# A four-layer attention kernel: the opening is rearranged, three biases move into columns, and the attention values are taken 64 queries at a time

## The chip, the cores and the metric

The kernel runs on one core of a Trainium2 chip. The metric is the device time of one execution in microseconds (us). The engines are named as the profile names them: PE is TensorE (PEld its weight loads), DVE is VectorE, ACT is ScalarE, POOL is GpSimd, SP is SyncE, which here only issues transfers.

## What is computed

`x` is 16 batches of 64 tokens with 128 features; `ctx_1024` is a second sequence of the same shape. Four blocks follow each other, all with 16 heads of 8 features, in f32:

```
L0: x = ln1(x + selfattn(x));  x = ln2(x + crossattn(x, ctx, every 4th key));  x = ln3(x + W2 gelu(W1 x + b1) + b2)
L1: q = x Ws + bs;  kv = ctx Wt + bt (keys are also the values);  a = attn(q, kv, masked) Wo + bo
    x = ln(x + [x, a] Wu + bu)
L2: x = ln(x + causal attention of x over ctx);  x = x + W2 gelu(W1 x + b1) + b2
L3: x = x + ( relu(q k)^2 in a band around ctx_index, divided by its floored sum ) v Wo,  q and k from rms-normed x and ctx
```

The kernel calls the five attentions sa, ca, l1, l2 and l3, and the two feed-forward parts f and g.

## The kernel before

The 1024 tokens are cut into four groups `g` of 256 (4 batches). A group has one PSUM bank, `bank[g]`, for everything but scores, and all groups share a four-bank tile `score`. There is no loop over layers. A table `SCHEDULE` lists some 700 steps as `step/layer/group/part`; every engine walks the whole table and does the steps that are its own, waiting on semaphores for what a step reads. So the table sets the order on each engine, and an engine that waits at one step does nothing of the next.

For one attention and group the steps are: `k`, `q`, `v` (PE, projections), `k_kept`, `q_kept` (ACT, bias added and copied to SBUF), `k_heads` and `q_heads` (DVE, four copies with the other heads masked out), `s` (PE, scores with queries on the partitions), `max` (DVE, row maxima), `max_parts` (DVE, the maxima split into two bf16 parts), `m` and `m_row` (PE, ACT: transposed), `t` (PE, the transposed scores, with the maxima subtracted through the `sel` matrix), two `exp` (ACT), two `av`, `divide` (DVE), `flip` and `attT` (transposed back), `z` (PE, output projection and residual, centred), `var`, `rstd` (ACT, POOL), `scale`, `flip_x`, `ln`.

`av` is the function `attend` (L494 on). Probabilities lie in SBUF with keys on the 128 partitions (two batches by the trick of alternating heads) and are the stationary operand; the values, with a column of ones for the denominator, are the moving one: 2 heads of 9 columns, 18 in all. A half of 256 tokens has 16 heads and 2 batches `x` of 64 queries, and each 64 are taken in two pieces `hf` of 32, so one matmul loads a 128x32 block and writes 32 partitions of the bank. One `av` step is 32 such matmuls; each f32 matmul appears as two in the trace, so 64 rows. There are 32 such steps in sa, l1, l2 and l3, and in ca four of 16 matmuls (32 rows) with 72 moving columns.

Three output biases are added in odd ways. `weights(3)` multiplies them through the output matrices into `shift` (three columns: sa, ca, f) and `row` (one row, l1). POOL adds `shift` to the layer's input x in place (`shifted`, 12 operations) before `z` reads it; for l1 a matmul of a row of ones with `row` (f32, 256 columns) opens each `z`.

The opening: SP issues x of group 0, the bias table V, three weight matrices, then x of groups 1 to 3 in one transfer; ACT issues the first two matrices. PE does 6 warm-up matmuls (`WARM`) and four more ahead of the first `s`. POOL zeroes the three value buffers `v_ext` one at a time, each inside its step `v_base`.

Of the kernel before, what the change touches and what calls it, by code (L numbers as in the profile page):

```python
# [10 lines left out]
R = 4  # L11
# [29 lines left out]
WARM = (6, 4)  # L41
# [7 lines left out]
SHIFT = {"sa": 0, "ca": 1, "f": 2}  # L49
W_BANK = {0: 3, 1: 2, 2: 3, 3: 3}  # L50
# [19 lines left out]

def own_readers(k):
# [23 lines left out]
k_heads/sa/3 weights_kept//3/2 m_row/sa/2 exp/sa/0/1 k/l1/1 k_kept/l1/1 t/sa/1 exp/sa/1/1 v/ca/1 av/sa/0/1 v_base/ca
v_even/ca/1 exp/sa/1 patterns divide/sa q_heads/sa/2 ctx_ms weights//3/3 s/sa/3 max/sa/3 weights_kept//3/3 av/sa/1
flip/sa k/ca/2 attT/sa max_parts/sa/3 k_heads/ca/2 k/l1 k_kept/l1 ctx_rs shifted/sa/1 shifted/sa/3 t/sa/2 exp/sa/2
q_heads/sa/3 av/sa/1/1 divide/sa/1 m/sa/3 m_row/sa/3 exp/sa/2/1 weights//2/1 flip/sa/1 shifted/sa z/sa var/sa
attT/sa/1 weights_kept//2/1 av/sa/2 rstd/sa t/sa/3 exp/sa/3 band z/sa/1 var/sa/1 k/ca/3 scale/sa k_heads/l1/1
flip_x/sa k_heads/ca/3 av/sa/2/1 ln/sa exp/sa/3/1 q/ca q_kept/ca rstd/sa/1 scale/sa/1 av/sa/3 flip_x/sa/1 ln/sa/1  # L100
divide/sa/2 v/ca flip/sa/2 v_even/ca attT/sa/2 q/ca/1 q_kept/ca/1 av/sa/3/1 divide/sa/3 s/ca max/ca shifted/sa/2
# [82 lines left out]
def build(nc, a, out):  # L184
# [3 lines left out]
    with ctx:  # L188
# [115 lines left out]
        def _(pe):  # L304
# [27 lines left out]
            def weights(i):  # L332
# [18 lines left out]
                else:  # L351
                    pe.wait_ge(sem("weights_kept"), nth("weights_kept", "", W_BANK[0], 0))
                    pe.wait_ge(sem("v_loaded"), 16)
                    for name, terms in (("sa", [("sa_vb", WC[:, WC_OF["sa"], :]), ("sa_ob", mat("center"))]),
# [3 lines left out]
                        for n, (b, m) in enumerate(terms):  # L358
                            mm(o[:, c:c + 1], m, col(b), start=n == 0, stop=n == len(terms) - 1)
# [732 lines left out]
```

## Time and profile before

| | us |
|---|---|
| median of 3 runs | 202.1 (201.26 to 202.43) |
| the profiled execution | 200.97 |
| its span in the trace | 199.0 |
| PE busy in the span | 180.7 (91%) |
| DVE, ACT, POOL busy | 131.7, 115.4, 47.6 |

The trace is of one execution, 1.1 us under the median. What lies around the span is 2.0 us. PE is busy nearly throughout; its idle time lies mostly in the opening.

### The profile page before, as it was taken

Reading aid. Unit: us, or ns where it says so; the run is one execution under the profiler, and the core shown is the slowest. Engines: PE = TensorE matmul, PEld = TensorE weight load, DVE = VectorE, ACT = ScalarE, POOL = GpSimd, SP = SyncE. Lnnn points to the kernel's source line nnn. Section 1 sums busy time; section 2 is a strip of 40 time slices with the busy share of each in tenths; the row PEclk is TensorE's granted clock in tenths of the full one; section 3 lists DMA queues with packets and bytes.
Section 4 is the critical chain, followed back from the end, with each engine's and each line's share of the span. In section 5 each row is a group of like instructions: output and inputs, shape, how many; then the busy total and the mean of one; then the engine's idle time right before and its main releaser. Section 6 shows DMA issues by size and latency. Waiting matters only on the chain.

```text
span 199.0 us, 10271 instructions
## 1 busy us (share of the span) xinstructions
PE 180.7 (91%) x4556; PEld 135.8 (68%) x4556; DVE 131.7 (66%) x250; ACT 115.4 (58%) x299; POOL 47.6 (24%) x73
## 2 busy tenths in 40 slices
PE   7693999989999999999999999898999999899863
PEld 3261768677878788778767667574667678777753
DVE  0799967986786873297367759634768156578770
ACT  2243348547485884667664566164597595554552
POOL 3793000943351167323101100011100102000000
PEclk9999799999999999999999999999999999999999
DMA  5992000000000000000000000000000000000102
GB/s 122 387 374 101 0 3 7 5 5 3 7 3 3 3 2 3 0 3 3 5 3 3 3 5 7 3 3 3 3 3 3 3 5 3 3 0 3 35 3 79
DMA packets 3899, 6.05 MB, mean 30 GB/s; under 512 B 528, under 2 KB 3216, under 8 KB 3600
## 3 DMA queue, kind: packets, MB, share of 16 engines
q1 hardware_dynamic: 3568, 5.23, 7.6%
q8 instruction: 36, 0.59, 1.2%
q10 hardware_dynamic: 288, 0.17, 0.3%
q14 instruction: 7, 0.06, 0.1%
HBM read 4.88 MB, written 0.52 MB: 27 GB/s over the span
## 4 chain that ended last, share of the span: by engine, by line
PE 67%; DVE 10%; issue 9%; ACT 5%; POOL 5%; DMA 3%; SPq 1%; POOLq 0%; DVEq 0%
PE bank L317 30%; PE score L320 21%; PE bank L320 10%; PE bank L533 4%; DVE m_col_sb L863 3%; DMA xa_sb<-in_xT 3%; ACT probs_sb L675 2%; DVE q_heads_sb L804 2%; POOL xa_sb L990 2%; DVE k_heads_sb L790 1%; DVE m_part_sb L870 1%; POOL xb_sb L990 1%; DVE probs_sb L850 1%; PE bank L443 1%; POOL rstd_sb L997 1%
## 5 line engine op out<-in xcount | busy, mean ns | idle before, releaser
L863 DVE TENSOR_REDUCE m_col_sb<-score 128x32 f32<-128x2048 f32 (+1 forms) x16 | 30.2, 1889 | 9.8 <-PE score L320 9.6
L675 ACT ACTIVATE probs_sb<-score 128x1024 f32<-128x1024 f32 (+1 forms) x28 | 26.4, 962 | 13.1 <-PE score L320 13.0
L317 PEld LDWEIGHTS bank<-v_ext_sb,probs_sb 128*32 128x32 f32 x2176 | 22.7, 110 | 9.6 <-issue 7.1
L317 PE MATMUL bank<-v_ext_sb,probs_sb 128*32 128x18 f32 (+1 forms) x2176 | 26.2, 189 | 1.9 <-DVE floor_sb L940 0.9
L995 POOL TENSOR_SCALAR vare_sb<-var_sb 128x2 f32<-128x2 f32 x20 | 5.5, 277 | 85.5 <-ACT att_sb L727 85.4
L317 PE MATMUL bank<-xa_sb,W_sb 128*128 128x256 f32 x62 | 18.2, 402 | 2.3 <-DMA xa_sb<-in_xT 1.6
L320 PE MATMUL score<-q_heads_sb,k_kept_sb 32*64 32x256 f32 x512 | 19.4, 386 | 0.9 <-DVE q_heads_sb L804 0.9
L927 DVE TENSOR_TENSOR att_sb<-bank,rstd_sb 128x256 f32<-128x256 f32 x20 | 8.4, 422 | 16.2 <-POOL rstd_sb L997 16.2
L740 ACT ACTIVATE hid_sb<-bank,V_sb 128x256 f32<-128x256 f32 x32 | 13.3, 471 | 8.6 <-PE bank L317 8.5
L320 PE MATMUL score<-k_heads_sb,q_kept_sb 32*64 32x256 f32 x384 | 14.3, 390 | 4.2 <-DVE m_col_sb L863 3.2
L727 ACT ACTIVATE att_sb<-bank 128x128 f32<-128x128 f32 x40 | 10.7, 276 | 10.7 <-PE bank L320 10.4
L533 PE MATMUL bank<-W_sb,att_sb 128*128 128x128 f32 x80 | 15.7, 283 | 1.1 <-DVE att_sb L890 0.8
L804 DVE TENSOR_TENSOR q_heads_sb<-q_kept_sb,small_sb 128x1024 f32<-128x1024 f32 x12 | 14.6, 1220 | 3.1 <-ACT q_kept_sb L686 3.0
L997 POOL TENSOR_TENSOR rstd_sb<-vare_sb,half_sb 128x2 f32<-128x2 f32 x20 | 14.3, 717 | 1.7
L317 PEld LDWEIGHTS bank<-xa_sb,W_sb 128*128 128x128 f32 x62 | 10.4, 193 | 5.9 <-issue 3.8
L790 DVE TENSOR_TENSOR k_heads_sb<-k_kept_sb,small_sb 128x1024 f32<-128x1024 f32 x11 | 13.5, 1235 | 1.1 <-ACT k_kept_sb L697 1.0
L317 PE MATMUL bank<-xb_sb,W_sb 128*128 128x256 f32 x48 | 13.8, 396 | 0.4 <-ACT xb_sb L732 0.2
L320 PEld LDWEIGHTS score<-k_heads_sb,q_kept_sb 32*64 32x64 f32 x384 | 7.5, 131 | 8.7 <-DVE m_col_sb L863 3.9
L320 PEld LDWEIGHTS score<-q_heads_sb,k_kept_sb 32*64 32x64 f32 x512 | 12.0, 131 | 2.1 <-issue 1.8
L659 ACT ACTIVATE v_ext_sb<-bank 64x128 f32<-64x128 f32 x32 | 8.8, 274 | 7.8 <-PE bank L317 7.2
L533 PEld LDWEIGHTS bank<-W_sb,att_sb 128*128 128x128 f32 x80 | 9.2, 142 | 5.3 <-DVE att_sb L890 2.1
L850 DVE SCALAR_TENSOR_TENSOR probs_sb<-score,band_sb 128x256 f32<-128x256 f32 x32 | 11.1, 416 | 2.2 <-PE score L320 2.2
(130 smaller groups left out, 354.2 us busy)
## 6 DMA issues: line engine op xcount, KB each, us to landing
W_sb<-in_mats SPq DMA_DIRECT2D x1, 1088.0 KB, 7.8
W_sb<-in_mats SPq DMA_DIRECT2D x1, 1024.0 KB, 9.9
ctxT_sb<-in_ctxT SPq DMA_DIRECT2D x1, 512.0 KB, 5.7
cn_sb<-in_ctx SPq DMA_DIRECT2D x1, 512.0 KB, 11.1
hid_sb<-in_idx SPq DMA_DIRECT2D x1, 512.0 KB, 6.5
out<-attT_sb SPq DMA_DIRECT2D x4, 128.0 KB, 1.8
xa_sb<-in_xT SPq DMA_DIRECT2D x1, 384.0 KB, 5.1
W_sb<-in_mats SPq DMA_DIRECT2D x1, 192.0 KB, 4.4
```

The source lines that it names most:

```text
L317: return pe.matmul(o, l, r, start=start, stop=stop)
L320: return pe.matmul(o, l, r, start=start, stop=True, skip_group_check=True)
L533: last = pe.transpose(o[:, j * 128:(j + 1) * 128], att[:, g, j, :], mat("ident"))
L659: last = act.activation(dst[:, :, 1 - f, :, 0:DH], src[:, :, 1 - f, :].rearrange("p c (h n) -> p c h n", n=DH), ACT.Copy)
L675: act.activation(dst, src, ACT.Exp, scale=SCALE).then_inc(sem("exp"), 1)
L727: last = act.activation(att[:, g, j, :], bank[g][:, j * 128:(j + 1) * 128], ACT.Square, scale=D ** -0.5, accum_out=var[:, g, j:j + 1])
L740: last = act.activation(hid[:, cc, tok(g)], bank[g][:, c * GT:(c + 1) * GT], ACT.Gelu, bias=col(f"{name}_b1_{cc}"), scale=1.0)
L790: dve.tensor_tensor(k_heads[HEADS[name]][:, g, :, :], k_kept[KEYS[name]][:, g, :].unsqueeze(1).to_broadcast([128, HH, GT]), const("head"). ...
L804: last = dve.tensor_tensor(q_heads[:, g, :, :], src.unsqueeze(1).to_broadcast([128, HH, GT]), const("head").unsqueeze(2).to_broadcast([128 ...
L850: last = dve.scalar_tensor_tensor(p, src, 0.0, m, ALU.max, ALU.mult)
L863: dve.tensor_reduce(o, src, AX.X, ALU.max).then_inc(sem("max"), 1)
L997: pool.tensor_tensor(rstd[:, g, :], vare[:, g, :], half[:, 0:NJ], ALU.pow).then_inc(sem("rstd"), 1)
```

## The change

**Values.** The loop over `hf` is gone: one matmul loads 128x64 and writes 64 partitions, so a step has 16 matmuls (32 rows) where it had 32 (64 rows). The same in ca with its 72 columns.

```diff
                     for a_ in range(2):
                         for h in range(HH):
-                            for hf in range(2):
-                                for x in range(2):
-                                    c = 64 * x + 32 * hf
-                                    o = bank[g][c:c + 32, i * 144 + a_ * 72:i * 144 + a_ * 72 + 72]
-                                    last = mm(o.rearrange("p (e h n) -> p e h n", e=2, h=HH)[:, :, h, :],
-                                              p[:, i, x, a_, h, 32 * hf:32 * hf + 32],
-                                              ve[:, x, g * NJ + i, 8 * a_ + h:8 * a_ + 8:HH, :])
+                            for x in range(2):
+                                o = bank[g][64 * x:64 * x + 64, i * 144 + a_ * 72:i * 144 + a_ * 72 + 72]
+                                last = mm(o.rearrange("p (e h n) -> p e h n", e=2, h=HH)[:, :, h, :],
+                                          p[:, i, x, a_, h, :],
+                                          ve[:, x, g * NJ + i, 8 * a_ + h:8 * a_ + 8:HH, :])
```

**Bias columns.** l1's bias becomes a fourth column of `shift`; a new `weights(4)` turns it, split into three bf16 parts, into `row` (3x128 bf16), and carries the ca and f shifts through the next matrices. DVE makes `moved` of it: biases of `ln` (sa, ca), of the f hidden layer and of ca's q. ACT adds them in operations that it does anyway, so POOL's `shifted` remains for sa only.

```diff
-SHIFT = {"sa": 0, "ca": 1, "f": 2}
+SHIFT = {"sa": 0, "ca": 1, "f": 2, "l1": 3}
+MOVED = ["sa_lb", "ca_lb", "f_b1_0", "f_b1_1", "f_b1_2", "f_b1_3", "ca_qb"]
...
-                                        ("f", [("f_b2", mat("center"))])):
+                                        ("f", [("f_b2", mat("center"))]),
+                                        ("l1", [("l1_ob", WC[:, WC_OF["l1_upd"], :]), ("l1_ub", mat("center"))])):
...
-                    mm(o[0:1, 128:256], col("l1_ob"), WC[:, WC_OF["l1_upd"], :], stop=False)
-                    last = mm(o[0:1, 128:256], col("l1_ub"), mat("center"), start=False)
...
+                    pe.transpose(o[0:3, 0:64].bitcast(BF), row_part[:, :], identb[:, :])
+                    for c in range(F_CHUNKS):
+                        mm(o[:, 128 + c:129 + c], mat(f"f_w1_{c}"), shift[:, SHIFT["f"]:SHIFT["f"] + 1])
+                    last = mm(o[:, 132:133], mat("ca_q"), shift[:, SHIFT["ca"]:SHIFT["ca"] + 1])
...
                     mm(bank_[:, 0:GT].rearrange("p (j d) -> p j d", j=NJ), ones_row[:, :],
-                       row[:, :].unsqueeze(1).to_broadcast([1, NJ, 128]))
+                       row[:, :].unsqueeze(1).to_broadcast([3, NJ, 128]))
...
+                elif i == 3:
+                    l1 = o[:, SHIFT["l1"]:SHIFT["l1"] + 1]
+                    dve.tensor_copy(shift[:], o[:, 0:len(SHIFT)])
+                    for c, n in enumerate(["sa_lb", "ca_lb"]):
+                        dve.tensor_tensor(moved[:, c:c + 1], col(n), o[:, 1 + c:2 + c], ALU.add)
+                    dve.tensor_copy(row_part[:, 0:1], l1).then_inc(sem("row_part"), 1)
...
+                    last = dve.tensor_tensor(row_part[:, 2:3], row_rest[:], row_part[:, 1:2], ALU.subtract)
```

**Opening.** x of group 1 gets its own transfer, third on SP; the first two matrices come in two transfers on ACT. The four warm-up matmuls ahead of the first `s` are gone. All zeroing comes first, one value buffer on DVE and two on POOL. `max_parts` multiplies by a column of minus ones, a tensor by tensor operation where a tensor by scalar one stood. In sa, ACT takes both halves of the values (`v_first`, `v_odd`), where DVE took one (`v_even`).

```diff
+            sp.dma_start(x_buf[0][:, tok(1)], a["xT"][:, tok(1)]).then_inc(sem("x_second"), 16)
             sp.dma_start(W[:, SA_MATS:FIRST_MATS, :], a["mats"][:, SA_MATS:FIRST_MATS, :]).then_inc(sem("w1_loaded"), 16)
-            sp.dma_start(x_buf[0][:, GT:TOK], a["xT"][:, GT:TOK]).then_inc(sem("x_loaded"), 16)
+            sp.dma_start(x_buf[0][:, 2 * GT:TOK], a["xT"][:, 2 * GT:TOK]).then_inc(sem("x_loaded"), 16)
...
-            busy(WARM[0])
+            busy(WARM)
             for step, name, g, i in ORDER:
-                if (step, name, g) == FIRST_S:
-                    busy(WARM[1])
...
+            dve.memset(v_ext[0][:], 0.0).then_inc(sem("v_zero_0"), 1)
...
-                dve.tensor_scalar(m_part[:, g, :, :, 0:HH], src, -1.0, None, ALU.mult).then_inc(sem("max_hi"), 1)
+                dve.tensor_tensor(m_part[:, g, :, :, 0:HH], src, minus[:, :].unsqueeze(2).unsqueeze(3).to_broadcast(
+                    [128, NJ, R, HH]), ALU.mult).then_inc(sem("max_hi"), 1)
...
+            pool.memset(v_ext[1][:], 0.0).then_inc(sem("v_zero_1"), 1)
...
+            pool.memset(m_part[:], 0.0).then_inc(sem("ones_ready"), 1)
+            pool.memset(v_ext[2][:], 0.0).then_inc(sem("v_zero_2"), 1)
```

**Order.** The whole table `SCHEDULE` is another one; its first lines:

```diff
-k/sa ones v_base/sa q/sa q_kept/sa k_heads/sa k_kept/sa sel q_heads/sa k/sa/1 k_kept/sa/1 k_heads/sa/1 s/sa max/sa
+v_base/ca sel k/sa k_heads/sa q/sa q_kept/sa k/sa/1 q_heads/sa s/sa k_kept/sa k_kept/sa/1 k_heads/sa/1 max/sa k/sa/3
...
```

PE from its first matmul to the first transposed scores, before. `xa` is x, `k_heads` times `q_kept` is `s`, `W` times `xa` is a step `v`, `m_part` is a step `m`, `sel` opens `t`:

```order
L317 MATMUL bank3<-warm_sb 128x512 x4
L320 MATMUL score<-k_heads0_sb,q_kept_sb 64x256 x16
L317 MATMUL bank1<-xa_sb,W_sb 128x256
L317 MATMUL bank2<-xa_sb,W_sb 128x256
L317 MATMUL bank3<-xa_sb,W_sb 128x256
L317 MATMUL bank2<-xa_sb,W_sb 128x256
L320 MATMUL score<-k_heads0_sb,q_kept_sb 64x256 x16
```

And now, from the same place, the key projection of group 1 on:

```order
L334 MATMUL bank1<-xa_sb,W_sb 128x256
L337 MATMUL score<-k_heads0_sb,q_kept_sb 64x256 x16
L334 MATMUL bank3<-xa_sb,W_sb 128x256
L334 MATMUL bank2<-xa_sb,W_sb 128x256
L334 MATMUL bank1<-xa_sb,W_sb 128x256
L334 MATMUL bank3<-xa_sb,W_sb 128x256
L334 MATMUL bank0<-W_sb,xa_sb 128x128 x2
L334 MATMUL bank1<-W_sb,xa_sb 128x128 x2
L334 MATMUL bank3<-W_sb,xa_sb 128x128 x2
L337 MATMUL score<-k_heads0_sb,q_kept_sb 64x256 x16
L334 MATMUL bank2<-xa_sb,W_sb 128x256
L334 MATMUL bank3<-W_sb 128x128 x5
```

The four warm-up matmuls no longer stand ahead of the first `s`; three value projections have moved ahead of the second `s`, and the five products of `weights(0)` (bank3 from W alone), which stood behind the first `t`, ahead of it and of the third `s`.

DVE in the opening, before, from its first to its third maximum (`m_col` is `max`, `m_part` is `max_parts`):

```order
L863 TENSOR_REDUCE m_col_sb<-score 128x32
L790 TENSOR_TENSOR k_heads_sb<-k_kept_sb,small_sb 128x1024
L870 TENSOR_SCALAR m_part_sb<-m_col_sb 128x8x4
L872 TENSOR_TENSOR m_part_sb<-m_col_sb,m_part_sb 128x8x4
L863 TENSOR_REDUCE m_col_sb<-score 128x32
L826 COPY v_ext_sb<-bank 64x4x4x8 x2
L870 TENSOR_SCALAR m_part_sb<-m_col_sb 128x8x4
L872 TENSOR_TENSOR m_part_sb<-m_col_sb,m_part_sb 128x8x4
L826 COPY v_ext_sb<-bank 64x4x4x8 x2
L863 TENSOR_REDUCE m_col_sb<-score 128x32
```

And now:

```order
L907 TENSOR_REDUCE m_col_sb<-score 128x32
L834 TENSOR_TENSOR k_heads_sb<-k_kept_sb,small_sb 128x1024
L907 TENSOR_REDUCE m_col_sb<-score 128x32
L914 TENSOR_TENSOR m_part_sb<-m_col_sb,minus_sb 128x8x4
L917 TENSOR_TENSOR m_part_sb<-m_col_sb,m_part_sb 128x8x4
L914 TENSOR_TENSOR m_part_sb<-m_col_sb,minus_sb 128x8x4
L917 TENSOR_TENSOR m_part_sb<-m_col_sb,m_part_sb 128x8x4
L790 COPY WC_sb<-bank 128x512
L907 TENSOR_REDUCE m_col_sb<-score 128x32
```

The second maximum follows the key copies directly, the value copies are gone from this stretch, and the copy of `weights(0)` has come in.

## Rows read from the trace of the kernel before

**Rows 1.** The page: busy time by engine, and the last chain by engine

```profile
PE 180.7 (91%) x4556; PEld 135.8 (68%) x4556; DVE 131.7 (66%) x250; ACT 115.4 (58%) x299; POOL 47.6 (24%) x73
PE 67%; DVE 10%; issue 9%; ACT 5%; POOL 5%; DMA 3%; SPq 1%; POOLq 0%; DVEq 0%
```

**Rows 2.** Stretches: us, busy time of each engine, granted clock, DMA share, GB/s

```profile
0.00:23.03 23.03, 16.74 (x147) 9.92 (x147) 16.94 (x19) 8.05 (x20) 12.04 (x19) 0.93 0.61 212
23.03:199.00 175.97, 163.92 (x4411) 125.87 (x4410) 114.72 (x232) 107.32 (x279) 35.56 (x54) 1.00 0.02 7
...
19.40:22.80 3.40, 3.40 (x28) 2.37 (x12) 3.28 (x6) 1.21 (x4) 0.00 (x0) 0.50 0.00 0
```

**Rows 3.** The chain that ended last, opening: start, us, what

```profile
2.10 5.07 DMA xa_sb<-in_xT
...
13.41 2.47 DVE m_part_sb L870
...
18.67 1.41 PE score L320 x32
```

**Rows 4.** The timeline of PE, opening: start, us, engine, line, what, idle before

```profile
7.30 0.67 PE L317 MATMUL bank<-xa_sb,W_sb 128*128 128x256 f32 x2 [1.59 <-DMA xa_sb<-in_xT]
...
8.77 1.12 PE L320 MATMUL score<-k_heads_sb,q_kept_sb 32*64 32x256 f32 x32
...
18.67 1.41 PE L320 MATMUL score<-k_heads_sb,q_kept_sb 32*64 32x256 f32 x32 [3.24 <-DVE m_col_sb L863]
...
23.03 0.43 PE L320 MATMUL score<-m_row_sb,sel_sb 8*64 8x128 bf16 x32
```

**Rows 5.** The timeline of DVE, opening

```profile
6.32 1.23 DVE L804 TENSOR_TENSOR q_heads_sb<-q_kept_sb,small_sb 128x1024 f32<-128x1024 f32 x1
...
12.20 1.22 DVE L790 TENSOR_TENSOR k_heads_sb<-k_kept_sb,small_sb 128x1024 f32<-128x1024 f32 x1
13.33 2.55 DVE L870 TENSOR_SCALAR m_part_sb<-m_col_sb 128x32 bf16<-128x32 f32 x1
...
19.13 0.18 DVE L870 TENSOR_SCALAR m_part_sb<-m_col_sb 128x32 bf16<-128x32 f32 x1
```

**Rows 6.** Transfers: KB, us from issue to landing

```profile
xa_sb<-in_xT SPq DMA_DIRECT2D x1, 384.0 KB, 5.1
...
xa_sb<-in_xT SPq DMA_DIRECT2D x1, 128.0 KB, 2.7
```

**Rows 7.** Groups by shape: busy us, mean ns of one, idle before

```profile
L317 PE MATMUL bank<-v_ext_sb,probs_sb 128*32 128x18 f32 x2048 | 23.5, 187 | 1.9 <-DVE floor_sb L940 0.9 <-ACT probs_sb L675 0.6 <-ACT probs_sb L720 0.3
L317 PEld LDWEIGHTS bank<-v_ext_sb,probs_sb 128*32 128x32 f32 x2176 | 22.7, 110 | 9.6 <-issue 7.1 <-DVE floor_sb L940 1.2 <-ACT probs_sb L720 0.4
...
L320 PEld LDWEIGHTS score<-q_heads_sb,k_kept_sb 32*64 32x64 f32 x512 | 12.0, 131 | 2.1 <-issue 1.8
...
L320 PEld LDWEIGHTS bank<-WC_sb,attT_sb 128*128 128x128 f32 x48 | 7.3, 192 | 0.0
...
L320 PE MATMUL score<-m_row_sb,sel_sb 8*64 8x128 bf16 x384 | 5.4, 220 | 0.7 <-DVE q_heads_sb L804 0.4 <-DVE m_col_sb L863 0.2
...
L317 PE MATMUL bank<-V_sb,W_sb 128*128 128x1 f32 x6 | 0.9, 250 | 0.0
```

**Rows 8.** The timeline of PE: runs of one shape

```profile
25.83 0.74 PE L317 MATMUL bank<-v_ext_sb,probs_sb 128*32 128x18 f32 x64
...
31.88 0.58 PE L317 MATMUL bank<-V_sb,W_sb 128*128 128x1 f32 x4
...
57.11 0.71 PE L317 MATMUL bank<-v_ext_sb,probs_sb 128*32 128x72 f32 x32
...
103.11 0.69 PE L317 MATMUL bank<-row_sb,ones_row_sb 1*128 1x256 f32 x2
```

**Rows 9.** POOL's additions to x, and who waited for them

```profile
L990 POOL TENSOR_SCALAR xa_sb<-xa_sb,shift_sb x8: 917/932/1632, 36.9 to 89.3; 128x256 f32<-128x256 f32 x8
...
  PE bank L320: 0.5, 1
```

More of the change, by code:

```diff
@@ L95 @@
[L95 to L99, printed above, removed]
@@ new lines @@
+flip_x/sa exp/sa/2/1 av/sa/2 m_row/sa/3 divide/sa/1 flip/sa/1 attT/sa/1 q_heads/sa/3 ln/sa band av/sa/2/1 z/sa/1
+v_base/l1 q/ca var/sa/1 divide/sa/2 t/sa/3 q_kept/ca k/ca/3 rstd/sa/1 scale/sa/1 exp/sa/3 v/ca shifted/sa/2
+flip/sa/2 k_heads/ca/3 v_even/ca exp/sa/3/1 flip_x/sa/1 av/sa/3 ln/sa/1 attT/sa/2 s/ca max/ca max_parts/ca q/ca/1
+q_kept/ca/1 av/sa/3/1 s/ca/1 divide/sa/3 m/ca max/ca/1 max_parts/ca/1 m_row/ca z/sa/2 var/sa/2 flip/sa/3 attT/sa/3
+ctx_scale t/ca v/l1 v_even/l1 exp/ca m/ca/1 m_row/ca/1 shifted/sa/3 z/sa/3 t/ca/1 v_odd/l1 var/sa/3 exp/ca/1
@@ new lines @@
+ln/ca/1 divide/ca/2 flip/ca/2 attT/ca/2 h/f/0/1 h/f/1 gelu/f/0/1 v_even/ca/3 av/ca/3 divide/ca/3 k/l2 gelu/f/1
+key_mask v/l1/2 h/f/1/1 k_kept/l2 gelu/f/1/1 v_even/l1/2 v_odd/l1/2 z/f var/f k_heads/l2 rstd/f k_heads/l1/2 z/ca/2
+var/ca/2 flip/ca/3 attT/ca/3 z/f/1 scale/f rstd/ca/2 scale/ca/2 var/f/1 rstd/f/1 flip_x/f ln/f flip_x/ca/2
+k_heads/l1/3 ln/ca/2 z/ca/3 q/l1 scale/f/1 h/f/2 flip_x/f/1 var/ca/3 rstd/ca/3 q_kept/l1 s/l1 scale/ca/3 ln/f/1
+q/l1/1 max/l1 flip_x/ca/3 gelu/f/2 h/f/2/1 q_heads/l1 max_parts/l1 ln/ca/3 q_kept/l1/1 h/f/3 s/l1/1 max/l1/1
@@ new lines @@
+gelu/f/2/1 max_parts/l1/1 z/f/2 m/l1 gelu/f/3 h/f/3/1 m_row/l1 var/f/2 rstd/f/2 gelu/f/3/1 m/l1/1 m_row/l1/1
+scale/f/2 t/l1 exp/l1 z/f/3 exp/l1/0/1 flip_x/f/2 ln/f/2 k/l2/1 q_heads/l1/1 var/f/3 k_kept/l2/1 k_heads/l2/1 av/l1
+rstd/f/3 t/l1/1 exp/l1/1 ctx_rows//1 ctx_normed//1 q/l1/2 q_kept/l1/2 scale/f/3 av/l1/0/1 divide/l1 flip_x/f/3
+av/l1/1 exp/l1/1/1 flip/l1 attT/l1 s/l1/2 q_heads/l1/2 k/l2/2 ln/f/3 k_kept/l2/2 q/l1/3 q_kept/l1/3 max/l1/2 z/l1
+av/l1/1/1 divide/l1/1 max_parts/l1/2 var/l1 ctx_rows//2 ctx_normed//2 s/l1/3 rstd/l1 scale/l1 max/l1/3 q_heads/l1/3
@@ L234, in build @@
         half = sb("half", [128, 8])
+        minus = sb("minus", [128, 1])
         warm = sb("warm", [128, 512], BF)
@@ L257, in build, with bias @@
         score = ctx.enter_context(nc.psum_tensor("score", [128, 4, 512], F))
+        def bias(n):
+            return moved[:, MOVED.index(n):MOVED.index(n) + 1] if n in MOVED else col(n)
         def const(n):
```

201 lines of the change are left out of this document (107 added, 94 removed).

## The prediction

> **What bounds the kernel now.** I read the busy times first: PE is at 91%, no other engine over 66%, and the last chain is 67% PE [rows 1]. Then two stretches, split where the first transposed scores (`t` of sa, group 0) start at 23.03 us [rows 2]. Before it PE is idle for 23.03 - 16.74 = 6.3 us; behind it, for 175.97 - 163.92 = 12.05 us in 176, in gaps under 1 us. So behind the opening the time is PE's work plus some 7% of waits, and a microsecond of PE work added there costs nearly one. In the opening the chain is another: it runs through the transfer of x (groups 1 to 3), through DVE's maxima and a `max_parts` operation of 2.47 us, and PE waits 3.24 us for a maximum [rows 3, 4]. Behind that wait PE ran at 0.50 of the clock, that is 1.2 GHz, from 19.4 to 22.8 us [rows 2]; before the wait and after 22.8 it ran at 2.4.
>
> **The values, the term that decides.** An `av` step is 64 matmuls, first start to end 0.74 us [rows 8]; the last takes 0.187 [rows 7], so the 63 steps between starts take 0.553, or 0.035 us for a round of four (one for each quarter of the array's columns). What sets a round? Two other runs answer. `V` through a matrix is a 128-column load and one moving column: four in 0.58, less the last one's 0.25, is 0.11 us each. The `sel` matmuls [rows 4] load 64 columns on each of eight parts of the array: 32 in 0.43, less 0.22, is 31/8 rounds in 0.21, or 0.054 a round. So a part can take a new block every 0.035, 0.054 and 0.11 us for 32, 64 and 128 columns: near enough in proportion to the columns loaded. The loads' own durations, 110, 131 and 192 ns [rows 7], step the same way. The `sel` case has 128 moving columns too, which could hide a shorter load; the other two have hardly any, and a straight line between them puts 64 columns at 0.035 + 0.075/3 = 0.060, so 0.057 is taken.
>
> Blocks of 64 queries are two to a round, not four, and a step still has 16 rounds (8 heads and column halves, two f32 passes, of both `x` together). New step: 16 x 0.057 = 0.91 us of starts, old 16 x 0.035 = 0.56. That is **+0.35 us** for each step though half the instructions are gone. The same columns are loaded, with half of them at a time. Of 32 such steps none is hidden from PE, whose queue is in order: 32 x 0.34 = **+10.9 us** of PE work. In ca the moving block of 72 columns sets the round: 0.71 us less a tail of about 0.2 over 8 rounds is 0.06 [rows 8], above 0.057 already; 0 there.
>
> Bounds: if an `av` step cost by instruction (0.0088 us each) the new one would be 0.28, -0.28 x 32 = -9 us. If load and moving pass did not overlap at all, a round would add the moving pass (36 column passes at 2.4 GHz, 0.015), 0.072: +0.6 x 32 = +19 us. I take +10.9, since the nearest rows, on both sides in columns, agree.
>
> On the lower bound there is a rule. The old step shows starts 0.0088 us apart on average [rows 7, 8]. The Trainium skill (TensorE: Matmul & The Clock Gate, "Wait — 56ns, not 53.3ns?") has start-to-start never below about 25 ns however few columns move, which would be a price by instruction: estimated by that page, 64 matmuls would take 1.6 us and 32 take 0.8, a gain of 25 us in all. The row speaks against it wherever the array is split, by a factor of three, so it is a rival with a small chance (below), and the sum goes by the rows.
>
> **The opening.** I replay it from durations in the rows. Group 1's x came with 384 KB, 5.1 us after an issue at 2.10 [rows 3, 6]; alone it is 128 KB, 2.7 us when it was first, issued at about 1.6: there by 4.5. So `k` of group 1 follows `q` at about 5.7 instead of 7.30, and the first `s`, with no warm-up matmuls before it, starts when `k_heads` is there, about 6.4 instead of 8.77 [rows 4]. DVE then runs without a gap: `q_heads` to 7.55 [rows 5], `k_heads`/1 to 8.8, maximum to 11.1, `k_heads`/2 (1.22) to 12.3, second maximum (2.29) to 14.6, two pairs of `max_parts` at about 0.4 to 15.4, one copy of 512 columns 0.7 to 16.1, third maximum to 18.4. `max_parts` was 2.55 us when POOL was zeroing and copying beside it and 0.18 when POOL was still [rows 5]; the other form and the earlier zeroing both should give the short one. `t` starts at 18.5 instead of 23.03: -4.5. Ahead of it PE now has also done the five products of `weights(0)`, 1.3 us of work that stood behind it: -1.3. PE's work up to there is some 10 us in 12.8, gaps under 1 us, so I expect no fall of the clock; the 1.7 us that the low clock cost (half of 3.4) are inside the 4.5. In return ACT has 8 more value copies of 0.27 and the eight squares of ctx ahead of the first `exp`, which comes about 0.3 late. Sum **-5.8 us**. Bounds: -2 (the `max_parts` stay long, or POOL's queue is late with the ones column of the value buffers, on which ACT's copies and all behind them on ACT wait), and -7.5 (6.3 idle, 1.7 of clock, 1.0 of warm-up, less what the first transfers cost anyway).
>
> **The bias columns.** `weights(3)`: two row products go, two one-column products (four instructions of 0.11) come; `weights(4)` adds five products, ten instructions, and a small transpose: together about **+1.2** on PE. The row of ones in l1: two f32 instructions over 256 columns [rows 8] become one bf16, about -0.3 in each of four: **-1.2**. DVE gets some ten operations of 0.15 to 0.2, one a chain of four that each wait for the last; queued behind it are the key and query copies of groups 3 and 2. PE has `t`/1, `av` and projections to do meanwhile: 0, up to +1 without them. POOL's additions for ca and f (8 of 12, 0.93 each) go; PE waited for any of them 0.5 us in the whole trace [rows 9], and that in sa, where they stay and now are ready earlier: at most -0.5. ACT's new waits (`ln`, `gelu`, `q_kept` on weights(3) and (4)) are for things long done.
>
> **What the longer steps hide.** 12 us of PE's idle time lie behind the opening. Some of it is waiting for DVE or ACT work that started before an `av` step, and a longer step covers it; the new order also shifts every gap, either way. With POOL's 0.5 I take **-1.5**, bounds +2 and -5.
>
> **Sum**, against the profiled 200.97: 201.0 + 10.9 - 5.8 + 1.2 - 1.2 - 1.5 = 203.6. The median is 1.1 above that execution, and I carry most of this: 204.7, rounded up for DVE's ten small operations to **204.9**.
>
> **Rivals.**
> (a) *Instructions set the price of `av`.* Place: 32 steps. For: half the instructions; in the second half of a step nothing says that starts are not bound by supply. Against: 0.11 us for a 128-column load with one moving column. Price -9 instead of +10.9; without the hidden waits 185, and as DVE's and ACT's waits then open, 185 to 192. This is the case on the other side: the change as a whole breaks even when a step grows by (5.8 + 1.5 + 0)/32 = 0.23 us, a round of 0.049; below that it is faster. Chance 0.08.
> (b) *The new order and the longer steps swallow more idle time* (6 to 7 of the 12 us, or the opening gives 7.5): 199 to 201.5. For: the gaps are many and small. Against: a longer step covers a gap only where it lies between the wait and what the wait is for. Chance 0.15.
> (c) *The opening does not give what it should*: one of the waits named above, or another fall of the clock to 1.2 GHz for a gap of 2 to 3 us: 207 to 210. Chance 0.13.
> (d) *Loads and moving passes do not overlap with two parts*: 210 to 213. Chance 0.04.
> The forecast has 0.60.
>
> **Range and chances.** 200.3 to 209.0 leaves out (a), (d) and the ends of (b) and (c), 0.18 in all. A measurement tells about 0.5%, 1 us, from no change. Faster than 201.1: (a) and a part of (b), 0.15. Within 1 us: 0.12. Slower: 0.73.
>
> **What would show it.** In the new profile: an `av` run of 32 rows that takes about 1.08 us (0.91 and a tail of 0.18) where 64 took 0.74; the group's busy time near 34 us instead of 23.5; the weight loads 128x64 near 135 ns. `t` starting at 18 to 19 us; no stretch at 0.50 behind 6 us; `max_parts` near 0.2. PE's busy time up by 8 to 9. Wrong would be: an `av` run under 0.7 us (then (a)), or `t` later than 20.5 us (then (c)).

## The result, and the profile after

The change made the kernel a little faster, where I had forecast slower.

| | median us | runs | lowest to highest |
|---|---|---|---|
| before, beside it | 201.97 | 20 | 199.08 to 205.28 |
| changed | 201.07 | 20 | 199.01 to 206.86 |

The ratio changed/before is 0.992 [0.9892, 0.9949]. Ratios leave out runs that lie over 1.5% above the fastest of their kernel while medians are of all runs, so the two can disagree where TensorE's clock varies from run to run, as it does here (last section). The profiled execution of the changed kernel took 200.1 us (span 198.3), 0.9 below the 200.97 of before.

The page of the changed kernel: busy time by engine, TensorE's clock in 40 slices, the queue that brings instructions, the last chain by engine, and the value steps' loads and matmuls (columns as in [rows 1, 7]).

```profile
PE 190.0 (96%) x3471; PEld 149.9 (76%) x3471; DVE 129.6 (65%) x251; ACT 117.0 (59%) x307; POOL 38.3 (19%) x65
...
PEclk9999987999999999999999999999999999999957
...
q8 instruction: 28, 0.46, 0.9%
...
PE 87%; DVE 6%; issue 2%; DMA 2%; ACT 1%; ACTq 0%
...
L334 PEld LDWEIGHTS bank<-v_ext_sb,probs_sb 128*64 128x64 f32 x1088 | 35.5, 140 | 7.1 <-issue 5.8
```

PE does 1085 matmuls fewer than in [rows 1] and is busy 9.3 us longer. The chain went from 67% PE to 87%, and its "issue" part, time in which the engine that the chain runs through waited for nothing that the profile shows, from 9% to 2%. I read over this 9% before.

Two stretches of the changed kernel, split where the first transposed scores start, as [rows 2] does; then one near the end.

```profile
0.00:18.32 18.32, 15.16 (x157) 10.22 (x157) 15.41 (x15) 11.35 (x38) 9.51 (x18) 1.00 0.81 268
18.32:198.30 179.98, 174.81 (x3317) 139.71 (x3317) 114.19 (x237) 105.68 (x271) 28.78 (x47) 0.97 0.02 6
...
187.00:190.50 3.50, 3.50 (x97) 3.50 (x96) 1.30 (x5) 1.36 (x3) 0.00 (x0) 0.77 0.04 12
```

Against [rows 2], the opening is 23.03 - 18.32 = 4.7 us shorter; behind it PE is busy 174.81 - 163.92 = 10.9 us longer and idle 179.98 - 174.81 = 5.2 us where it was idle 12.05, so 6.9 less. The sum is -4.7 + 10.9 - 6.9 = -0.7, the difference of the spans. So the price of the values and the gain of the opening came about near the forecast, and the idle time went down by much more than my 1.5 us.

PE's timeline, changed kernel: an early value step (one step is 32 rows), and one run of three steps near the end. Then the same engine's busy groups of the values by shape.

```profile
22.27 1.11 PE L334 MATMUL bank<-v_ext_sb,probs_sb 128*64 128x18 f32 x32
...
186.97 3.77 PE L334 MATMUL bank<-v_ext_sb,probs_sb 128*64 128x18 f32 x96
```

```profile
L334 PE MATMUL bank<-v_ext_sb,probs_sb 128*64 128x18 f32 x1024 | 36.0, 214 | 0.3 <-ACT probs_sb L695 0.3
...
L334 PE MATMUL bank<-v_ext_sb,probs_sb 128*64 128x72 f32 x64 | 2.9, 232 | 0.0
```

From its first start to its last, a step that nothing holds up takes 0.903 us, where it took 0.555: +0.348, and 32 of them are 11.1 us. Up to the start of the instruction behind it, it is 1.044 against 0.669, +0.375 or 12.0 us in all, less where steps follow each other directly. The last run is longer than three steps because it falls into a stretch at 1.2 GHz.

And what PE waited for in the whole execution, before and after: line, releaser, us in total, times, longest. Before:

```profile
PE score L320 <- DVE q_heads_sb L804: 1.3, 3, 0.5
PE score L320 <- issue: 1.2, 2, 0.9
...
PE bank L320 <- issue: 0.8, 1, 0.8
PE bank L317 <- issue: 0.8, 1, 0.8
```

Changed:

```profile
PE score L337 <- DVE m_col_sb L907: 1.8, 4, 0.6
...
PE score L337 <- issue: 0.3, 1, 0.3
```

Behind the first transposed scores, the waits of 0.2 us and more add up to 2.8 us for "issue" and 5.4 for other engines before, and to 0.3 and 2.2 after. The rest of the idle time is in gaps too short for the list, and in the tail behind PE's last matmul.

### The profile page after: what moved, and what is told of

The parts are those of the page before. It is cut to its first block, busy times and chain, and to the rows that moved or that the text cites. A ratio compares the mean times of both kernels' runs of the same rounds, so it can differ in the third digit from the quotient of the medians.

```text
span 198.3 us, 8112 instructions
## 1 busy us (share of the span) xinstructions
PE 190.0 (96%) x3471; PEld 149.9 (76%) x3471; DVE 129.6 (65%) x251; ACT 117.0 (59%) x307; POOL 38.3 (19%) x65
## 4 chain that ended last, share of the span: by engine, by line
PE 87%; DVE 6%; issue 2%; DMA 2%; ACT 1%; ACTq 0%
PE bank L334 43%; PE score L337 22%; PE bank L337 13%; PE bank L553 6%; DVE m_col_sb L907 5%; DMA small_sb<-in_small 2%; ACT probs_sb L695 1%; PE bank L467 1%; PE bank L660 1%; DVE k_heads_sb L834 1%; PE bank L415 1%; DVE q_heads_sb L848 1%; PE bank L616 0%; ACTq L698 0%; DVE att_sb L935 0%
## 5 line engine op out<-in xcount | busy, mean ns | idle before, releaser
L334 PEld LDWEIGHTS bank<-v_ext_sb,probs_sb 128*64 128x64 f32 x1088 | 35.5, 140 | 7.1 <-issue 5.8
L334 PE MATMUL bank<-v_ext_sb,probs_sb 128*64 128x18 f32 (+1 forms) x1088 | 38.9, 215 | 0.3 <-ACT probs_sb L695 0.3
L1038 POOL TENSOR_SCALAR vare_sb<-var_sb 128x2 f32<-128x2 f32 x20 | 6.4, 319 | 116.0 <-ACT att_sb L752 115.9
L334 PE MATMUL bank<-xa_sb,W_sb 128*128 128x256 f32 x62 | 17.6, 400 | 0.2
L553 PE MATMUL bank<-W_sb,att_sb 128*128 128x128 f32 x80 | 16.5, 295 | 0.1
L933 DVE RECIPROCAL rden_sb<-bank 128x32 f32<-128x32 f32 x16 | 5.7, 356 | 14.8 <-PE bank L334 14.8
L848 DVE TENSOR_TENSOR q_heads_sb<-q_kept_sb,small_sb 128x1024 f32<-128x1024 f32 x12 | 14.9, 1239 | 0.0
L679 ACT ACTIVATE v_ext_sb<-bank 64x128 f32<-64x128 f32 x40 | 10.9, 273 | 1.9 <-PE bank L334 1.2
L748 ACT ACTIVATE attT_sb<-bank 128x256 f32<-128x256 f32 x16 | 6.1, 382 | 9.6 <-PE bank L553 9.5
```

The costliest lines, as they stand in the source:

```text
L334: return pe.matmul(o, l, r, start=start, stop=stop)
L553: last = pe.transpose(o[:, j * 128:(j + 1) * 128], att[:, g, j, :], mat("ident"))
L679: last = act.activation(dst[:, :, e, :, 0:DH], src[:, :, e, :].rearrange("p c (h n) -> p c h n", n=DH), ACT.Copy)
L848: last = dve.tensor_tensor(q_heads[:, g, :, :], src.unsqueeze(1).to_broadcast([128, HH, GT]), const("head").unsqueeze(2).to_broadcast([128 ...
L1038: pool.tensor_scalar(vare[:, g, :], var[:, g, :], EPS, None, ALU.add).then_inc(sem("var_eps"), 1)
```

## The experiments

**Which part gives what.** My first suspicion was that the opening gave its gain, that the values cost 11 us, and that something in the new order paid it back. The rival was that the values themselves cost less in time than in PE's busy time. Four kernels took the change apart.

The changed kernel with the old blocks of 32 queries, everything else as changed:

```diff
-                            for x in range(2):
-                                o = bank[g][64 * x:64 * x + 64, ...]
+                            for hf in range(2):
+                                for x in range(2):
+                                    c = 64 * x + 32 * hf
+                                    o = bank[g][c:c + 32, ...]
```

> The changed kernel with the values taken 32 queries at a time again (64 rows a step), everything else as changed. Both theories: a step costs 0.55 us of starts again instead of 0.90, PE's work falls by 32 x 0.35 = 11 us. Theory O (the new order has little waiting in itself; PE's idle time behind the first t stays near 5 us): 11 us faster than the changed kernel, 188 to 190 us, ratio to before 0.94. Theory P (the longer steps covered the waits, which reopen to some 11 us): 4 to 5 us faster than the changed kernel, 194 to 196 us, ratio 0.965. If steps did not set the time at all: no change against the changed kernel.

199.49 us (6 runs), ratio to before 0.9864 [0.9807, 0.9921]. No theory forecast that: theory O had 188 to 190, theory P 194 to 196. With 11 us of loads taken back the kernel is 3 us faster than the changed one beside it (202.4, below) by the medians, and not faster by the ratios (0.9864 against 0.9805). PE is busy 178.7 us, as it should be, so it stands still the more. Its waits, and its timeline in two places:

```profile
PE bank L334 <- issue: 3.7, 6, 1.5
PE score L337 <- issue: 2.8, 4, 1.6
PE score L337 <- DVE m_col_sb L911: 2.1, 4, 0.7
PE bank L337 <- issue: 1.9, 1, 1.9
```

```profile
46.08 0.37 PE L337 MATMUL score<-kc_kept_sb,q_kept_sb 32*64 32x64 f32 x14
48.01 0.39 PE L337 MATMUL score<-kc_kept_sb,q_kept_sb 32*64 32x64 f32 x18 [1.56 <-issue]
...
187.16 1.04 PE L334 MATMUL bank<-v_ext_sb,probs_sb 128*32 128x18 f32 x71
188.91 1.23 PE L334 MATMUL bank<-v_ext_sb,probs_sb 128*32 128x18 f32 x121 [0.71 <-issue]
```

8.4 us go to "issue", where the changed kernel has 0.3. And they lie in the middle of runs: 14 of 32 small matmuls are done, then nothing for 1.56 us, then the other 18, which read the same tiles. No wait, no engine and no buffer stands between the fourteenth and the fifteenth. What is left is that the fifteenth was not there to be issued.

The kernel before, with blocks of 64 and nothing else (the values' part of the change, alone):

```diff
-                            for hf in range(2):
-                                for x in range(2):
-                                    c = 64 * x + 32 * hf
+                            for x in range(2):
```

> The kernel before with the one edit of 64-query blocks, its own order and opening. Both theories: 0.90 us of starts a step instead of 0.55. Theory O: idle time behind the first t falls only from 12 to about 10, so 209 to 212 us, ratio 1.045. Theory P: it falls by 6 to 7 us, so 206 us, ratio 1.02.

204.91 us (6 runs), ratio 1.0112 [1.0046, 1.0178], under what both theories gave (206, and 209 to 212). The blocks alone, in the old order, cost 1.1%, some 2.3 us, a fifth of the 11 us that they add to PE. Its list of waits has no line with "issue" (2.8 us before), and the first transposed scores start at 21.37 and not 23.03. In this list the largest entry behind them is

```profile
PE score L320 <- DVE q_heads_sb L800: 0.9, 2, 0.5
```

with others of 0.2 to 0.7: 3.8 us in all, where it was 5.4. So -2.8 for "issue", -1.6 for what the longer steps hide (my -1.5), and -1.7 in an opening that this edit doesn't touch and that moves from run to run: together 6.1 of the 11. The rest of the difference between the two profiles isn't separated.

The changed code under the old order, twice. The first attempt put the second product of the bias columns directly behind the first:

```diff
-... max/sa/3 weights_kept//3/3 av/sa/1 flip/sa k/ca/2 ...
+... max/sa/3 weights_kept//3/3 weights//3/4 weights_kept//3/4 av/sa/1 flip/sa k/ca/2 ...
```

> The changed kernel's code with the order table of before (the new steps put in: weights 4 behind weights 3, the identity copy where the ones stood, no shifts for ca and f). It has the own transfer, zeroing first, bias columns, 64-query blocks. Theory O (the order carries the gain): 205 to 208 us; the opening gives 2 to 3 us of its 5.8 without the order. Theory P: 200 to 202 us, as the changed kernel.

206.28 us (6 runs), ratio 1.026 [1.0202, 1.0318]. That is the range of theory O, but not for its reason. It has a gap of 3.35 us at 29.35, in which PE waits for `row_part`, the chain of small DVE operations of the bias columns: an artefact of where I put the step. It shows what this chain costs if PE has nothing else to do: the "0, up to +1" of the prediction's bias part is too small as an upper bound, and in the changed kernel's own place the cost is hidden. Moved behind `weights(2)`:

> The changed kernel's code with the old order table, as newcode_oldorder_64, where weights(4) stood directly behind weights(3) and PE waited 3.35 us for DVE's parts of the bias; here it stands some 25 steps later. If the order as such is worth little: 200 to 202 us, as the changed kernel. If it is worth something beside that misplaced step: 203 to 205 us.

200.51 us (10 runs), ratio 0.9927 [0.9878, 0.9977]: the changed kernel's time (0.992). Under the old order, with the new opening, it goes as well. So the new table of order is worth nothing that can be told here, and the suspicion of "something in the new order" falls.

The changed kernel again, as the fourth of the first set, for the clock and the opening:

> The changed kernel unchanged, for the same chip and rounds as the three others: 199 to 202 us, ratio 0.985 to 0.995 to before. Its profile shows whether the two stretches at 0.50 of the clock (28.4 to 31.9 us and 188.9 to 195.7 us, while PE was never idle for long) come again at the same places.

202.4 us (12 runs), against 202.08 of before (17 runs); ratio 0.9805 [0.9743, 0.9867] by the rule on runs above. Both lie outside what was expected, on opposite sides. The medians say no difference here, and the ratio says 2%. I take from it that the change is worth between nothing and 2%, depending on what the clock does. The stretches at 1.2 GHz came again in the same parts of the kernel, not at the same places: 23.0 to 26.4, 29.8 to 33.3 and 190.3 to 193.7.

**Is it the supply of instructions?** By now the theory is: PE executes its instructions faster than they arrive. What brings them is in the page, in the line of queue 8: before 36 transfers of 0.59 MB together, 16 KB each, and 28 in the changed kernel. Each brings 256 instructions if one is 64 bytes, and the counts bear this out: in all fourteen traces the number of transfers is PE's loads and matmuls over 256, rounded up (9112 and 36, 6942 and 28, 7966 and 32 in the mixed kernel below). In the traces they take 0.9 to 1.5 us each and never start less than 3.3 us apart: 256 in 3.3 us are 78 an us.

The traces have the times of these transfers, and they tie the stalls to them. In all fourteen together PE has 37 "issue" waits of 0.25 us or more. 36 of them end 1.2 to 1.6 us after a transfer of queue 8 has landed (2.2 to 2.8 us after it started); the other is one of 0.3 us in the kernel before. Of the 82 waits of that length for anything else, after the first 20 us of each trace, 9 end in this band. And the eleven "issue" waits of 1 us and more all stand behind some 250 instructions that PE went through in 2.0 to 2.7 us.

Stretches of 10 us of the 32-query form (after_32) come up against the rate. Columns as in [rows 2], from the changed opening with blocks of 32:

```profile
31.00:41.00 10.00, 8.77 (x396) 7.10 (x402) 8.88 (x14) 4.67 (x14) 3.27 (x5) 1.00 0.02 4
113.00:123.00 10.00, 9.17 (x385) 6.29 (x376) 6.98 (x11) 4.17 (x9) 0.00 (x0) 1.00 0.02 6
```

and the same two of the changed kernel:

```profile
31.00:41.00 10.00, 10.00 (x241) 8.13 (x226) 7.64 (x11) 4.16 (x10) 2.16 (x3) 0.96 0.02 4
113.00:123.00 10.00, 10.00 (x265) 7.58 (x254) 6.86 (x11) 4.33 (x10) 0.00 (x0) 1.00 0.02 4
```

Loads and matmuls together are 798 and 761 in 10 us in the first, with PE idle 1.2 and 0.8 us; 467 and 519 in the second, with PE never idle. A value step in blocks of 32 is 128 instructions in 0.56 us, three times that rate; where several come close to each other, PE is through with the instructions that it has before the next transfer is in.

The test of "issue" as supply under the old order: the changed code under the old order with blocks of 32.

```diff
-                                for x in range(2):
+                            for hf in range(2):
+                                for x in range(2):
```

> The same code and old order with 32-query blocks: what opening and bias columns give alone, with the old steps. By the prediction's opening term, 196 us. If opening gains are given back later, as waits: 198 to 200 us.

199.57 us (4 runs), ratio 0.9894 [0.9822, 0.9965]. "Issue" is 7.5 us, where the kernel of before has 2.8 with nearly the same order of the steps:

```profile
PE bank L333 <- issue: 3.2, 4, 1.2
PE score L336 <- issue: 2.8, 4, 1.3
PE score L336 <- DVE m_col_sb L910: 1.9, 3, 1.1
```

So it isn't the new order that makes the stalls. Three of them stand at the same instructions as in the kernel before (some 5610, 6110 and 9090 loads and matmuls in), and four of the five new ones lie before 56 us, behind the shorter opening. I read this as PE's work lying more densely there, which uses up the instructions sooner, and as the place where much of the gain of the opening goes in the 32-query form; no run separates it further.

Then fewer instructions. The first takes most of them out of the values: in sa, l1, l2 and l3, one matmul of 72 columns for each half of the heads and block of 64 queries, where there were four of 18 (all eight heads then use the first one's probabilities, so three quarters of the attention values are left out; it is the time that is read).

```diff
-                        for h in range(HH):
-                            for x in range(2):
...
-                                          p[:, i, x, a_, h, :],
-                                          ve[:, x, g * NJ + i, 8 * a_ + h:8 * a_ + 8:HH, :])
+                        for x in range(2):
...
+                                      p[:, i, x, a_, 0, :],
+                                      ve[:, x, g * NJ + i, 8 * a_:8 * a_ + 8, :].rearrange("p h n -> p (h n)"))
```

> The changed kernel with the values cut short: one matmul of 72 moving columns for each 64 queries and half of the heads instead of four of 18, all with the first head's probabilities, so that three quarters of the attention values are not computed rightly; a step is 8 rows, about 0.25 us of starts instead of 0.90, 21 us less PE work in all. If the time behind the opening is set by PE's work (as the prediction had it): 178 to 182 us. If shorter steps only reopen waits for DVE and ACT (which 32-query blocks gave: PE's idle time behind the first t 12.3 us instead of 2.5, no faster profile): a floor near 195 us, with 20 us or more of idle time.

185.55 us (4 runs), ratio 0.9175 [0.9059, 0.9291], between the two theories. PE is busy 167.7 us, 22.3 less than in the changed kernel, and 14.9 of it came out of the span. Some 2.8 of both are clock (one stretch of 3.4 us at 1.2 GHz, not three; last section):

```profile
PE 167.7 (91%) x2703; PEld 124.9 (68%) x2703; DVE 128.7 (70%) x251; ACT 116.7 (64%) x307; POOL 38.2 (21%) x65
```

Its longest waits:

```profile
PE score L337 <- DVE q_heads_sb L846: 2.0, 2, 1.2
PE bank L551 <- DVE att_sb L970: 1.2, 2, 0.8
```

"Issue" stays at 0.2, and the waits for other engines grow from 2.2 to 9.4 us. So PE's work is worth some two thirds of its length when it goes, since the others are then late, and the value steps do hide those waits. The other direction: each value step of sa, l1, l2 and l3 twice.

```diff
-                    for a_ in range(2):
+                    for a_ in [0, 1, 0, 1]:
```

> The changed kernel with each step of the values done twice over (same result), 64 rows of 64-query blocks, 1.83 us of starts, 29 us more PE work. There are only 2.3 to 2.5 us of waits left behind the first t to cover, so both theories say that now the price is nearly full: 225 to 230 us, with 1 us of idle time left. Under 220 would mean that PE's queue isn't what orders the work.

240.67 us (4 runs), ratio 1.1838 [1.1661, 1.2015], where 225 to 230 was expected. The work is as it should be: 1.836 us from first to last start of a doubled step, 0.933 more than 0.903 and 29.9 us in all; "issue" 0, other waits 2.2 as before. What goes beyond the expectation is the clock:

```profile
23.40:40.50 17.10, 17.10 (x220) 13.10 (x217) 6.85 (x16) 2.86 (x5) 5.59 (x4) 0.50 0.01 2
224.80:235.00 10.20, 10.20 (x147) 10.16 (x143) 1.94 (x6) 1.15 (x3) 0.00 (x0) 0.50 0.02 5
```

With a third stretch of 6.8 us that is 34.1 us at 1.2 GHz, 24 more than in the changed kernel. By the 1.4 us that 3.4 us of such a stretch cost (last section), these are 10 us, and the time without them is some 230.5 us, at the top of what was expected. The cost in PE's work, then, is as the prediction had it.

**A kernel between the two.** If PE is short of array time with blocks of 64, and of instructions with blocks of 32, the best lies between. Each pair of value steps takes its first with blocks of 64 and its second with 32 (ca stays at 64):

```diff
-                            for x in range(2):
-                                o = bank[g][64 * x:64 * x + 64, ...]
+                            for hf, n in ((0, 64),) if i == 0 else ((0, 32), (1, 32)):
+                                for x in range(2):
+                                    c = 64 * x + 32 * hf
+                                    o = bank[g][c:c + n, ...]
```

> The changed kernel with blocks of 64 queries in the first step of each pair and of 32 in the second (same result). Theory I (with 32-query blocks PE lacks instructions: 9112 instead of 6942 of them, in the trace idle time before PE that no wait explains, 8.4 us against 0.3): half the extra instructions are gone and half the extra load time, PE's unexplained idle 1 to 3 us, PE's work 5.5 us under the changed kernel: 195 to 197.5 us, faster than both pure forms. Theory P (longer steps cover waits for DVE and ACT): as both pure forms, 199 to 201 us.

**193.29 us** (6 runs), ratio to before 0.9603 [0.9547, 0.9658], where the supply theory said 195 to 197.5 and faster than both pure forms. It is 4% faster than the kernel before; against the changed kernel it is 4% by the medians and 2 to 3% by the ratios (0.9805 and 0.992). Part of that is clock, which the forecast left out: the profiled run has one stretch of 3.4 us at 1.2 GHz and the changed kernel's three, some 2.8 of the 5.6 us between them (194.5 and 200.1). Where the whole run was at full clock, it took 192.5 to 193.0 us (3 runs), and the 32-query form 197.6 (1 run).

```profile
PE 182.6 (95%) x3983; PEld 141.7 (74%) x3983; DVE 130.3 (68%) x251; ACT 116.9 (61%) x307; POOL 38.0 (20%) x65
```

And of its waits, those with "issue":

```profile
PE score L337 <- issue: 0.5, 2, 0.3
PE bank L415 <- issue: 0.4, 1, 0.4
PE bank L334 <- issue: 0.3, 1, 0.3
```

Half the steps in blocks of 32 take 7.4 us off PE's busy time (16 x 0.348 = 5.6, and the rest mostly clock), and only 0.9 us of "issue" comes back of the 8.1 that all of them bring. So the stalls do not grow in proportion to the instructions added. One step on, with all of l2 in blocks of 32:

```diff
-                            for hf, n in ((0, 64),) if i == 0 else ((0, 32), (1, 32)):
+                            for hf, n in ((0, 64),) if i == 0 and name != "l2" else ((0, 32), (1, 32)):
```

> As after_mix (193.3 us), but the eight steps of l2 are all of 32-query blocks: four more steps at 0.56 us of starts instead of 0.90, 256 more PE instructions. If the supply has room in l2 once the rest is mixed: PE's work 1.4 us less, 191.5 to 192.5 us. If l2 is where it is short (after_32 had a stall inside l2's values at 118.8 and one at 132 us): stalls of 1 to 3 us come back there, 193 to 195 us.

194.69 us (6 runs), ratio 0.9659 [0.9607, 0.9711] to the same kernel before. The second of the two outcomes named:

```profile
PE score L337 <- issue: 1.4, 2, 1.1
PE score L337 <- ACT probs_sb L697: 0.8, 1, 0.8
```

PE's busy time falls by another 0.9 us and a stall of 1.1 us opens in l2, at 152: no gain. The difference of the two ratios is half the width of their intervals, so which of them is faster isn't settled; that l2 does not bring the 1 to 2 us of its first outcome (191.5 to 192.5) is.

**One that did not tell.** If supply is short, taking instructions out elsewhere should end the stalls. In sa, l1 and l2 the matmuls that spread the maxima (`sel`, 32 in each `t`) were left out, so the maxima aren't subtracted there:

```diff
-                if name != "l3":
-                    for h in range(1 if name == "ca" else HH):
+                if name == "ca":
+                    for h in range(1):
...
-                                           q_heads[rows_of(r), g, :, of_batch(b)], start=name == "l3" and j == 0)
+                                           q_heads[rows_of(r), g, :, of_batch(b)], start=name in ("l3", "sa") and j == 0)
```

with blocks of 32

> The changed kernel with 32-query blocks and without the matmuls that subtract the row maxima in sa, l1 and l2 (the maxima are still computed and laid out; the softmax is the same without them). It leaves out 12 runs of 32 matmuls, 768 PE instructions that take 0.26 us a run, 3.1 us of PE work. Theory I: it gains those 3.1 us and, since 768 of the 2176 instructions that 32-query blocks have over 64-query ones are gone, 2 to 4 us of supply stalls: 5 to 7 us under after_32 (199.5), so 193 to 195 us. Theory P: at most 3 us, 196.5 us or more.

and of 64:

> The changed kernel as it is, 64-query blocks, with the same matmuls left out. It has no stalls for instructions to lose (0.0 to 0.3 us), so theory I: it gains 2.5 to 3.5 us and no more, 196 to 198 us, and ends behind after_32_nosel though it was level with after_32. Theory P: the same gain as after_32_nosel has over after_32.

197.8 us (6 runs, 192.16 to 200.21) and 197.22 us (6 runs, 191.05 to 199.93). In the 32-query form "issue" stayed at 8.4 us although 768 instructions are gone. The expectation failed. By the traces it is not the number of instructions in the kernel that counts, but how fast PE goes through some 250 of them in a row. The nine stalls that this form has end 1.3 to 1.5 us after a transfer has landed, like the others, and one stands at a new place (97.8 us, 1.4). Why leaving out the `sel` matmuls thinned none of the dense stretches (they follow a wait for DVE in most places) is argued, not shown. The two kernels can't be compared with each other either. Each ran between a clock of 1.00 and one of 0.95, 8 to 9 us apart, and at 1.00 there is one run of each: 192.16 and 191.05.

## Why the prediction was wrong

One slip ahead of the terms: 201.0 + 10.9 - 5.8 + 1.2 - 1.2 - 1.5 is 204.6 and not 203.6, so these terms stand for a median of 205.9 and not 204.9. The slip brought the forecast nearer to the measurement, by luck. The terms are 4.5 us above the 200.1 of the profiled run.

- **The value steps, +10.9.** Right in mechanism and size: 0.903 us a step where 0.91 was worked out, +0.348 against +0.35, loads at 140 ns where 135 were expected, the group at 36.0 us against 34 (some of it run at 1.2 GHz). A part of the array takes a new block after a time that grows with the block's columns. Rival (a), price by instruction, is out for PE's array, and so is (d). The rule of the Trainium skill that the prediction weighed (TensorE: Matmul & The Clock Gate, "Wait — 56ns, not 53.3ns?") does not hold for a split array here: the old form's starts are 0.0088 us apart. The new one's, 0.903/31 = 0.029, lie above that bound and say nothing against it.
- **The opening, -5.8.** t at 18.31 (18.5 forecast); no low clock before it. The parts came by other routes than I gave them. The first `s` started at 6.31 behind `k_heads`, as forecast, but `k_heads` itself waited for a transfer that I had not followed: `small`, third on ACT's queue, now behind two transfers of matrices instead of one.

DVE's timeline, changed kernel, opening:

```profile
4.88 1.28 DVE L826 SCALAR_TENSOR_TENSOR k_heads_sb<-bank,V_sb,small_sb 128x1024 f32<-128x1024 f32 x1 [1.35 <-DMA small_sb<-in_small]
...
8.83 2.28 DVE L907 TENSOR_REDUCE m_col_sb<-score 128x32 f32<-128x2048 f32 x1
...
14.60 0.18 DVE L914 TENSOR_TENSOR m_part_sb<-m_col_sb,minus_sb 128x32 bf16<-128x32 f32 x1
```

`max_parts` took 0.18 us instead of 2.55. The start of t differs from run to run: 18.3 to 19.2 us in the seven profiles of kernels with this opening and order that have these matmuls.
- **The bias columns, +1.2 - 1.2.** The row of ones is four bf16 rows of 278 ns, 1.1 us, where it was eight f32 rows and 2.8: -1.7, a little more than forecast. DVE's chain is hidden where the change has put it, and costs 3.35 us where it is not.
- **What the longer steps hide, -1.5. This is the step that failed.** It came out at -6.9. The part that I meant, waits for DVE and ACT covered by longer steps, was sized well: 5.4 to 3.8 in the kernel before with the blocks alone. In the changed kernel the waits for others fell to 2.2, and those for "issue" from 2.8 to 0.3; the last 1.2 of the 6.9 is in gaps too short for the list. What I did not see is that some 2.5 of the 12 us of idle time was PE running out of instructions, which blocks of 64 end since the values need half as many. That is 2.5 of the 5.4 us that I missed; the waits for others fell 1.7 further than the 1.5, with the new order and the bias columns (3.6 are left in the changed kernel with blocks of 32). The row was there: three lines with "issue" in PE's list of waits. The 9% in the chain [rows 1] and the 7.1 us ahead of the loads of the values [rows 7] are poorer signs: the changed kernel, which has next to no such stalls, still has 5.8 us ahead of those loads, and the kernel with the short values 6% "issue" in its chain. I had rival (a) for a price by instruction but looked for it in the array alone, and there gave it 0.08. It lies ahead of the array.
- **The rest.** Not forecast was any stretch at 1.2 GHz, and the changed kernel has 10.2 us of them behind t. By the price of the last section that is +4.3 us in the profiled run; it took back most of what I missed. -5.4 (idle, beyond the 1.5), +4.3 and -0.2 (t at 18.3) make -1.3 of the -4.5 us between 204.6 and the 200.1 measured. The other 3 us are in terms of PE's busy time: -0.5 in the row of ones, the rest in parts that no run separates. So the lost clock hid most of the missed idle time: a kernel that kept its clock would have been further from the forecast.

Where the term's worth lies: without the blocks of 64, about half of the opening's gain is gone (0.9864, 2.7 us of 5.8), and the 32-query form stands still for 8.4 us, where the kernel before stood for 2.8. Against that form the blocks of 64 add 11.3 us to PE's busy time, 1.4 of it clock, and take 8.1 of "issue" and 1.4 of other waits. So the two forms are about level (profiled spans 198.3 and 197.7), and the kernel in between, which keeps half of the short loads and has 1.2 us of stalls, is the fastest of all.

## What to carry to other kernels

- Where PE's small matmuls stop inside a run that waits on nothing, count loads and matmuls there. This kernel's stream delivered 256 in 3.3 us at best, some 78 an us, and every stall of 1 us or more stood behind some 250 of them in 2.0 to 2.7 us; a mean over 10 us can hide such a stretch. Where it is dense, a form with fewer, longer instructions costs less than its busy time says.
- Such a choice need not be made for the whole kernel: one step in 64-query blocks and the next in 32 was worth 4% against the kernel before, when either form alone was within 2% of it.
- "Issue" in the list of waits is a term of the sum like any other. Price it before the change, and ask what a denser schedule will make of it.

## What the runs showed of the hardware

**Instructions arrive at a limited rate.** Transfers of 16 KB, one for each 256 of PE's loads and matmuls, 0.9 to 1.5 us each, never under 3.3 us apart, and stalls of PE of 0.3 to 1.9 us: 8.4 us in the 32-query form of the changed kernel, 7.5 under the old order, 2.8 before, 1.2 in the mixed one, 1.7 in the one with all of l2 in blocks of 32, and 0 to 0.3 in the 64-query ones. That supply is the cause rests on the stalls' ends (36 of 37 stand 1.2 to 1.6 us behind a landing), on their going with the instructions of the value steps, and on the mixed kernel, whose place ahead of both forms was forecast from it. No run changed the transfers themselves, and the one that removed other instructions did not lessen the stalls. The Trainium skill (Runtime: NRT & Kernel Launch, "Instruction fetch mechanics") has blocks of 16 KiB too, fetched ahead of execution, and says that the cost of going from one to the next is mostly hidden. In six of the traces here, with 1.2 to 8.4 us of stalls, it isn't.

**The clock falls while PE is busy.** In the kernel before, the 1.2 GHz stretch came 0.7 us behind a wait of 3.24 us [rows 2, 4]. In the changed one there are three of about 3.4 us, one in 28.4 to 31.9 and two in 188.9 to 195.7, and ahead of the last two PE has no gap (187.00 to 190.50 above: 3.50 us busy of 3.50). Over its 20 runs the time follows the mean granted clock: about 199 to 200 us at 0.974 to 0.983, 203.7 at 0.949, 206.8 at 0.933. A line through them gives 195 us at full clock, an estimate since none of the 20 ran there, and 1.4 us for each further 3.4 us at 1.2 GHz. This is most of the scatter of 199 to 207, as wide as the effects in question. The kernel with doubled value steps fell lowest (0.92 to 0.94), which points to those steps; but the 32-query form without `sel` also had runs from 1.00 to 0.955. Nor is it only the idle time: in the 32-query form both stretches start 0.2 to 0.5 us behind a stall of 1.5 us, but under the old order the same form had four stalls of 1.0 to 1.5 us and ran at full clock to its end. I did not find what sets it off.

**The more columns a part of the array loads, the longer its round.** 32, 64 and, in the prediction's rows, 128 columns: 0.035, 0.058 (0.903 us over 15.5 rounds) and 0.11 us a round, a little less than in proportion. The 64-column round took 0.058 with 18 moving columns and 0.054 with the 128 of the `sel` matmuls [rows 4], so the moving pass adds nothing that can be told here.
